# A four-layer cross-attention kernel: in the relative-position layer TensorE turns probabilities two half steps behind their scores instead of three

## The reference, cut to what matters

```python
q, k, v = projections, 16 heads of width 16          # per batch element: 512 x 16 a head
QEr  = einsum('bhsd,ld->bhsl', q, Er)                # relative-position scores, 512 x 512 a head
Srel = _skew(QEr)                                    # row s shifted so that column t is the distance s - t
attn = (einsum('bhsd,bhtd->bhst', q, k) + Srel) / sqrt(16)
attn = softmax(where(causal, attn, -inf))
out  = einsum('bhst,bhtd->bhsd', attn, v)
```

## Time and profile before

| | |
|---|---|
| time, median of 3 runs | 3734.76 us (3732.8 to 3737.67) |
| the profiled execution | 3726.14 us, span 3724.3 us |
| mean granted TensorE clock | 0.923 |
| busy of the span | PE 84%, DVE 66%, ACT 60%, POOL 30% |
| copies out of t_ps, L1148 | 512, 228.5 us, mean 484 ns |
| score units, L1158 | 512, 232.0 us, mean 485 ns |
| transposes, L1065 | 1280, 226.1 us |

### The profile page before, as it was taken

One profiled execution on the slowest core, in us unless ns is written; L12 is line 12 of the kernel. 1 busy time (PEld: TensorE's weight loads), 2 busy tenths in 40 slices (PEclk: granted clock), 3 DMA queues, 4 the chain that ended last, 5 costly groups with the idle time before them and its releaser, 6 DMA issues. The chain is left out here.

```text
span 3724.3 us, 67376 instructions
## 1 busy us (share of the span) xinstructions
PE 3116.7 (84%) x17249; PEld 1587.6 (43%) x17249; DVE 2443.1 (66%) x7452; ACT 2234.5 (60%) x3026; POOL 1134.4 (30%) x1290
## 2 busy tenths in 40 slices
PE   5999998787688888759968888887479999965997
PEld 3344432333333333126635555554234344334565
DVE  5777775887677677652227778777877777745431
ACT  2777777664499899931127666676547777840111
POOL 4444440000555555111123333321333122010332
PEclk8999999999899999969989989999589999975998
DMA  5323320001533343010039989996132221112332
GB/s 151 90 71 81 98 64 17 20 1 35 131 99 93 106 118 93 27 53 0 0 96 326 304 277 297 315 322 209 30 77 50 66 49 41 36 41 85 91 101 58
DMA packets 212160, 392.92 MB, mean 106 GB/s; under 512 B 24633, under 2 KB 76985, under 8 KB 211657
## 3 DMA queue, kind: packets, MB, share of 16 engines
q1 hardware_dynamic: 168777, 296.38, 28.5%
q10 hardware_dynamic: 36864, 83.90, 6.1%
q0 software_dynamic: 6144, 8.39, 1.3%
HBM read 189.88 MB, written 96.47 MB: 77 GB/s over the span
## 5 line engine op out<-in xcount | busy, mean ns | idle before, releaser
L506 DVE CUSTOM_DVE_ANT_0 A_sums<-A_ring_ps,A_bias 128x512 bf16<-128x512 f32 x1536 | 1035.8, 687 | 437.3 <-PE A_ring_ps L322 416.6
L569 ACT ACTIVATE A_probs<-A_p_ps 128x1024 f32<-128x1024 f32 x768 | 779.5, 1016 | 196.2 <-PE A_p_ps L337 109.7
L322 PE MATMUL A_ring_ps<-A_k_stack,A_q_stack 96*128 96x512 bf16 x1536 | 573.3, 390 | 99.0 <-DVE A_maxima L506 34.5
L554 ACT ACTIVATE A_p_ps<-A_biasT 128x1024 f32<-128x1024 bf16 (+1 forms) x512 | 525.8, 1027 | 52.4 <-ACT A_m_row L532 7.5
L337 PE MATMUL A_p_ps<-A_q_stack,A_k_stack 99*128 99x512 bf16 x1536 | 464.3, 384 | 41.1 <-ACT A_p_ps L554 35.5
L353 PE MATMUL A_oT_ps<-A_probs,A_v_aug 128*17 128x512 f32 x3072 | 410.9, 607 | 0.7 <-ACT A_probs L569 0.7
L322 PEld LDWEIGHTS A_ring_ps<-A_k_stack,A_q_stack 96*128 96x128 bf16 x1536 | 147.4, 97 | 603.3 <-DVE A_maxima L506 373.6
L1158 DVE CUSTOM_DVE_ANT_0 A_scores<-A_qk_ps,A_rel_in 128x384 f32<-128x384 f32 (+3 forms) x512 | 232.0, 485 | 81.8 <-PE A_qk_ps L1042 72.4
L1065 PE MATMUL A_t_ps<-ident,A_scores 128*128 128x128 f32 x1280 | 226.1, 298 | 57.2 <-DVE A_probsT L1148 46.9
L1213 ACT ACTIVATE A_rel_out<-A_rel_ps 128x1024 f32<-128x1024 f32 (+3 forms) x256 | 180.2, 704 | 144.7 <-PE A_rel_ps L1031 142.7
L1220 ACT ACTIVATE A_scores<-A_scores,A_nmax 128x384 f32<-128x384 f32 (+3 forms) x512 | 257.5, 555 | 7.1 <-DVE A_nmax L1158 6.8
(11 more groups left out here) (343 smaller groups left out, 5366.3 us busy)
## 6 DMA issues: line engine op xcount, KB each, us to landing
A_k_stack<-A_parts SPq DMA_DIRECT2D x192, 256.0 KB, 5.1
A_q_stack<-A_parts SPq DMA_DIRECT2D x192, 256.0 KB, 5.5
A_rel_dram<-A_rel_out ACTq DMA_DIRECT2D x64, 512.0 KB, 5.0
A_rel_in<-A_rel_dram SPq DMA_DIRECT2D x64, 512.0 KB, 5.1
A_rel_dram<-A_rel_out ACTq DMA_DIRECT2D x64, 384.0 KB, 4.5
A_rel_in<-A_rel_dram SPq DMA_DIRECT2D x64, 384.0 KB
A_ctxT<-in_ctxT SPq DMA_DIRECT2D x32, 512.0 KB, 6.5
A_mask_in<-in_mask SPq DMA_DIRECT2D x64, 256.0 KB, 4.5
```

Source lines behind the costliest of these rows:

```text
L322: nc.tensor.matmul(bank(*turn)[:, :], q_stack[0:KS, a_par, j * GH + i, t * P:(t + 1) * P], k_stack[0:KS, a_par, j * GH + i, :], start=True ...
L506: nc.vector.tensor_tensor_reduce(out=sums[:, i % NX, :], in0=bank("p1", s * GH + i)[:, :], in1=bias[:, t, :], scale=-1.0, scalar=3.4028235 ...
L554: nc.scalar.activation(p2_ps[half][:, :, :], turned, ACT.Copy).then_inc(seeded, 1)
L569: nc.scalar.activation(probs[:, s % 2 * 2 + half, :, :], p2_ps[half][:, :, :], ACT.Exp).then_inc(exp_done, 1)
```

## The change

One constant. Everything that is worked out from it (the half step that PE turns, L1057 to L1065, and the half step that DVE copies, L1141) moves with it; the order of the parts inside a half step, the numbers of buffers, and `PV_LAG` stay.

```diff
     LEAD = 4
-    TURN_LAG = 3
+    TURN_LAG = 2
     PV_LAG = 3
```

## The result

The changed kernel takes 3859.07 us, median of 4 runs (3856.62 to 3869.24), against 3733.78 us (3725.32 to 3737.67) for the kernel before; ratio 1.035, 95% interval 1.033 to 1.037. It is slower by 125 us. The forecast was slower by 81 us, 3815 us, in a range of 3780 to 3870. Direction, place and the new wait for PV were as forecast; the price came out half as large again.

What follows compares the result with a forecast made beforehand. DVE bounds the stage, PE close behind. Net 2.73 us a group, 87 us in 32 groups, less 6 us covered by the value bias: + 81 us, 3815 us; range 3780 to 3870, likeliest case 3787 to 3850.

Steps and rivals of the forecast that it cites:

- (a): DVE's wait for turned probabilities: PE turns what DVE copies at p - 1, before and after; no gain.
- (c): PE's wait for `t_ps` at odd half steps: PE stands through the first copy, losing slack; no second term for DVE.
- (b): DVE's copies at odd half steps wait for PV of the same half step; 4.43 us a group before hand-backs.
- The closed chain: At odd half steps: last score of p - 1, q·k product, PV, then copies; DVE stands still, so no gain.
- (d): PE's wait for the exponentials, which have one half step less; 1.7 us margin on the largest, costed at nothing.
- (e): DVE's wait before a score for the turning of p - 4 becomes looser; costed at nothing.
- The price of a plain group: Group without projections: 4.43 us of pushed copies less 1.7 us handed back, net 2.73 us.
- One price for both kinds of groups: Groups with and without projections both priced at net 2.73 us, 87 us in 32 groups.
- The clock rival: PE's small stands lower the stage's clock by 0.15, 34 us more, 3849 us; chance 0.09.
- Little is handed back: PE's stand makes its projections late, so the next even half step waits again for products; 3871 us, chance 0.10.
- The transfers set the pace: DMA stores and loads bound the stage, so a slower DVE hides behind them; about 3740 us, chance 0.07.
- faster: Earlier turning removes DVE's 42.5 us of waits for turned probabilities and PV costs nothing; 3692 us, chance 0.05.

Runs made afterwards that it cites:

- The unrolled pair: TURN_LAG = 3 (kernel before) and TURN_LAG = 2 (changed kernel), each with the loop over blocks 1 to 4 written out: 3703.75 and 3797.56 us.

## Why the prediction was right, and where its size was off

- The measured 3859 us lies in the range that was given, but above the likeliest case's own 3787 to 3850 us. It is inside only because the upper bound was set for rivals that did not happen, so that the range held is in part luck; the new wait, its place and its direction are not.
- (a), (c), no gain in the relation of turning and copying: right. PE's waits before L1065 for L1148 rose from 46.9 to 137.3 us, as (c) has it. With the wait for PV removed by buffers, TURN_LAG = 2 is within 0.3% of TURN_LAG = 3.
- (b), the wait for PV of the same half step: right, in classes 1 to 3; in class 0 it is 0.1 us. Two experiments remove it and one shortens it.
- The closed chain of (b): the engines do run one after the other, but the chain closes through L1041 only in class 2, where the second q·k product starts 0.07 us after the last score. In class 1 it starts 0.48 us after it, in class 3 0.29 us (medians outside the loop). What PE is at until then is the turning of the even half step: 8 transposes from 2629.10, where the last score ends at 2629.69, and 6 from 2638.33, where it ends at 2639.06. These turnings hang on DVE too, the one on the copy out of `t_ps` (0.20 us of waiting before 2629.10), the other on the q·k product before it (2638.04), which waits 0.20 us for DVE's score. The prediction counted this for class 1 (0.35 us). For class 3 it put the longer turning at nothing, since the q·k product "waits for DVE or ACT meanwhile"; in the changed kernel it does not.
- (d), the exponentials at nothing: no run isolates it. With buffers alone the total did not rise. But the sign "waits of L1065 for ACT's exponentials not up" was not met: 3.8 us in 3 waits of PE before, 9.0 us in 10 in the changed kernel (1981 us on).
- (e), stage end at nothing: the last group grew from 15.44 to 21.63 us, twice a plain group's price, with its clock at 0.68 where it was 0.89. The score's wait for the turning of p - 4 rose from 0.9 to 5.3 us. All 16 of these waits lie in the loop, and the unrolled kernel has none.
- The price of a plain group: 2.73 us forecast, 19.31 - 16.34 = 2.97 us measured. The stands were put at 1.58, 1.19 and 1.66 us (4.43) and were 1.72, 1.20 and 1.79 us (4.71). One term was short, the hand-over: taken as 0.07 us from the nearest row, a score to a product, it is 0.24 us from a PV's recorded end to a copy, 0.17 us more at each of three stands. That is 0.51 us, but the stands are only 0.28 us longer than forecast, so the other parts of the sum were 0.23 us too long. What reached the time is the 0.24 us of the plain group, 8 us in 32 groups. The two directions are not alike; the row that I took was the other direction. The Trainium skill, page "Perfetto Trace Analysis", section "Tensor Engine Instruction (MATMUL, LD_WEIGHTS)", has TensorE's semaphore update go out only when PSUM has acknowledged the last bytes. That agrees with the longer way from PE to DVE, though no run here takes the 0.24 us apart.
- "One price for both kinds of groups" and for all blocks: this is the step that was mis-sized. Outside the loop, block 5 grew by 13.4 us (forecast 4 x 2.73 - 0.84 = 10.1). In the loop, block 1 grew by 18.1 us. The unrolled pair measures the loop's part: 125 - 94 = 31 us of the 44 us by which the forecast fell short; of the remaining 13 us the plain group's 0.24 us is 8, and 5 are not taken apart. The plain groups that I read lay outside the loop, while half of the blocks lie within. The rows of a group with projections do come from the loop (block 3), but from the kernel before, so they could not show what the loop adds once DVE waits for PV in three of four odd half steps. The sign for these waits, 1.0 to 1.6 us each and 120 to 150 us in sum, was exceeded as well: up to 5.6 us each, 203 us in sum.
- The clock rival: small over the stage, not everywhere. The stage's clock fell from 0.93 only to 0.92 over 1955 to 2735 us. But it fell from 0.91 to 0.83 in block 3 and from 0.95 to 0.86 in block 7, and block 3 grew most of all, block 7 most of those outside the loop. A dip has a price, in the changed kernel 21.86 us for a group at 0.84 against 19.31 us at 1.00, but the unrolled kernel with TURN_LAG = 2 has fewer dips (0.96 over its stage, against 0.94 with TURN_LAG = 3) and still pays 94 us. At the loop's turn in the middle the changed kernel has a stretch at half clock, where the same turn before was at 0.67 (2195 to 2215 us):

```profile
2255.00:2275.00 20.00, 13.08 (x75) 8.39 (x76) 8.63 (x28) 6.62 (x12) 1.22 (x3) 0.50 0.66 191
```

  How much of the loop's 31 us goes by way of dips in its blocks and how much by dearer hand-overs is open: writing the loop out takes both away.
- "Little is handed back", 3871 us: nearer to the measured time than the forecast, but not the mechanism. 63 us were handed back, more than the 54 us forecast (32 x 1.7). It was the price that was larger: 203 us of waits where 136 were put.
- The transfers set the pace, and faster: excluded. The DMA share in a plain group fell from 0.92 to 0.84.

## What to carry to other kernels

In a software pipeline, a lag fixes not only when a thing is ready but which reader must be done before its buffer is written: with NP buffers, write down for each parity the half step whose reader frees the buffer. Here lag 3 has a reader one or more half steps back and lag 2 the reader of the very same half step. If that reader stands behind work that itself hangs on the waiting engine, the two engines run one after the other; then further buffers, or the reader moved as well, give the time back, and here the second gave more. And take the price of a hand-over from a row in the same direction, and in the same kind of code: in a hardware loop with counted waits it was 0.40 us, in written-out code 0.24 us.

## What the runs showed of the hardware that was not expected

- From the recorded end of a PE group (which the profile models) to the DVE instruction that waits for it: 0.24 us in written-out code with waits for constants, 0.40 us in the loop with waits for counted values. From DVE's score to PE's product, written out: 0.07 us where PE had nothing else to do.
- Two 128 wide score units of DVE that follow each other start 0.21 to 0.24 us apart in written-out code, with few exceptions, and 0.21 to 0.50 us apart in the loop. With 384 and 512 wide ones the loop makes no such difference.
- Writing the loop of one layer out saved 30 us of 3734 without any other change, in spite of more code. About 9 us of it are the loop's single turn.
